# A planned pipeline on one core: first parts ordered by urgency with quantising beside the first early part, four banks in the last back part, step sizes one after the other, long steps in halves

## What is computed

```python
x = x + layernorm(attention(layernorm(x)))   # 2 heads, relu on q, k, v and on the output
x = x + layernorm(moe(layernorm(x)))         # 8 experts of 176, top 2, and a shared one; SwiGLU
x = x + layernorm(mamba(layernorm(x)))       # d_inner 512, 16 states, grouped B and C, conv of 4 taps
x = x + layernorm(ffn(layernorm(x)))         # relu squared, hidden 1024, rms norm, ternary weights
# mamba: delta = softplus(dt @ W_dt.T + 2 * b_dt)
#        state = exp(delta * A) * state + (delta * u) * B ;  y = sum over states of C * state
#        y = (y + u * D) * silu(z) ;  out = y @ W_out.T
# ternary weight: per 64 numbers scale = mean |w|, q = clip(round(w / scale), -1, 1) * scale
```

## Time and profile before

| | us |
|---|---|
| median of 3 runs | 1946.99 (1944.04 to 1947.22) |
| profiled execution, its own time | 1944.15 |
| its span | 1942.4 |
| busy: PE, DVE, ACT, POOL | 1609.7, 1521.5, 1198.9, 1000.3 |
| preamble and early(0) | 97.4 |
| late(0), early(1), quantising | 145.2 |
| iteration 0 | 193.8 |
| iterations 1 to 5 | 1053.1 (210.6 each) |
| iterations 6 and 7 | 203.4 and 157.7 |
| back(7) alone | 91.8 |

### The profile page before, as it was taken

One profiled execution on the slowest core, in us unless ns is written; L12 is line 12 of the kernel. 1 busy time (PEld: TensorE's weight loads), 2 busy tenths in 40 slices (PEclk: granted clock), 3 DMA queues, 4 the chain that ended last, 5 costly groups with the idle time before them and its releaser, 6 DMA issues. The chain is left out here.

```text
span 1942.4 us, 22619 instructions
## 1 busy us (share of the span) xinstructions
PE 1609.7 (83%) x5868; PEld 716.1 (37%) x5948; DVE 1521.5 (78%) x2808; ACT 1198.9 (62%) x2035; POOL 1000.3 (52%) x772
## 2 busy tenths in 40 slices
PE   2266488878997899979998899889997999789856
PEld 0113123323452346333552345234633354235224
DVE  5384599979998898969897998889986878586920
ACT  4347765677669575857577766957685536743421
POOL 0100645594449544764459444964477445864720
PEclk9987689879998899979998999989997899799988
DMA  4010022322223222322232222322232223232300
GB/s 117 2 48 22 25 85 95 111 80 79 92 92 110 73 85 77 121 77 75 87 107 81 87 88 85 115 73 90 71 121 77 82 92 119 75 111 93 123 1 11
DMA packets 94601, 157.95 MB, mean 81 GB/s; under 512 B 10940, under 2 KB 23660, under 8 KB 94468
## 3 DMA queue, kind: packets, MB, share of 16 engines
q1 hardware_dynamic: 94468, 156.43, 24.4%
HBM read 143.83 MB, written 12.58 MB: 81 GB/s over the span
## 5 line engine op out<-in xcount | busy, mean ns | idle before, releaser
L1401 POOL TENSOR_TENSOR prod<-state,c_all 128x512 f32<-128x512 f32 x512 | 653.0, 1280 | 550.5 <-DVE state L1378 436.1
L1378 DVE TENSOR_TENSOR_SCAN state<-decay,ps_b 128x512 f32<-128x512 f32 x512 | 621.8, 1214 | 53.3 <-ACT decay L1121 30.2
L924 PE MATMUL ps_y<-prod,idf 128*128 128x512 f32 x1024 | 606.2, 685 | 18.2 <-DVE u L1391 9.7
L1121 ACT ACTIVATE decay<-delta,a_neg 128x512 f32<-128x512 f32 x512 | 362.7, 721 | 222.6 <-DVE state L1378 221.9
L1385 DVE TENSOR_TENSOR ps_b<-du,ps_b 128x512 f32<-128x512 f32 x512 | 349.1, 682 | 87.2 <-PE ps_b L917 86.4
L917 PE MATMUL ps_b<-b_rows,sel_b 48*128 48x512 bf16 x512 | 207.3, 408 | 74.5 <-DVE state L1378 72.7
L924 PEld LDWEIGHTS ps_y<-prod,idf 128*128 128x128 f32 x1024 | 174.3, 203 | 165.1 <-issue 107.3
L917 PEld LDWEIGHTS ps_b<-b_rows,sel_b 48*128 48x128 bf16 x512 | 47.1, 93 | 376.5 <-DVE state L1378 234.0
L793 PE MATMUL ps_x<-xT,w 128*128 128x512 bf16 (+1 forms) x386 | 130.4, 417 | 30.7 <-DVE arena_l L1284 12.0
L896 PE MATMUL ps_x<-arena_b,fcT 128*128 128x512 f32 x256 | 125.4, 613 | 6.2 <-ACT arena_b L1103 5.5
L709 PE MATMUL ps_x<-hT,win 128*128 128x512 bf16 (+1 forms) x449 | 114.5, 388 | 13.3 <-DVE arena_b L1350 6.8
(11 more groups left out here) (236 smaller groups left out, 2411.1 us busy)
## 6 DMA issues: line engine op xcount, KB each, us to landing
c_all<-c_rows SPq DMA_DIRECT2D x512, 256.0 KB
c_rows<-arena_l SPq DMA_DIRECT2D x32, 256.0 KB
out<-arena_b SPq DMA_DIRECT2D x8, 512.0 KB
x_in<-in_base SPq DMA_DIRECT2D x8, 256.0 KB
c_all<-in_winT SPq DMA_DIRECT2D x1, 1280.0 KB, 7.1
arena_b<-in_w_fc SPq DMA_DIRECT2D x1, 1024.0 KB, 5.8
arena_b<-in_w_proj SPq DMA_DIRECT2D x1, 1024.0 KB, 4.7
w<-in_w1T SPq DMA_DIRECT2D x1, 792.0 KB, 5.8
```

The source lines that it names most:

```text
L924: nc.tensor.matmul(ps_y[:], idf[:], prod[:, n % NP, :], start=(n % NST == 0), stop=(n % NST == NST - 1)).then_inc(reduced, 1)
L1121: nc.scalar.activation(decay[:, n % NDA, :], delta[:, slot(s, ct), :], ACT.Exp, scale=a_neg[:, ct, st:st + 1]).then_inc(decayed, 1)
L1378: nc.vector.tensor_tensor_scan(state[:, n % NS, :], decay[:, n % NDA, :], ps_b[:, n % NDB, :], 0.0, ALU.mult, ALU.add).then_inc(scanned, 1)
L1401: nc.gpsimd.tensor_tensor(prod[:, n % NP, :], state[:, n % NS, :], c_all[:, n % NC, :], ALU.mult).then_inc(multiplied, 1)
```

## The change

1. **First parts.** `together`, `in_slots` and `COST` are gone. early(0) runs alone as before, and from round 24 of its 106 on (17 behind the `divide` of its first norm) the 30 quantising rounds are put behind its rounds at equal distances. Both weights are loaded with the other weights, ahead of w1, w3 and w2, each into a buffer of its own. Then `weave` orders late(0) (urgency 1000) and early(1) (urgency 1) until `du 0` is over, and the rest of both goes into iteration 0 as *held* chains, where late(1) and early(2) may start only when both are over. That iteration has weights of its own (`FIRST`).
2. **Last back part.** In back(7) the products of `wout`, `f_turn`, `fc`, `proj` and `gram` go to four banks by turns (`back_bank`), and their waits are those for the copy four products back.
3. **Step sizes.** The order of the blocks becomes 0, 3, 1, 2 (`D_ORDER`), and each has nine rounds of its own (15 + 9 k) instead of chains that begin at rounds 14, 15, 17 and 18.
4. **Halves.** `proj`, `gram`, `fc`, `wout`, `x4`, `apply`, the `add` of GpSimd and `gate_root` become two steps each (`first_half`, `halved`), and so does the store. Between the halves the planner can put steps of other chains.
5. **Planner.** New `BUSY`, table loads counted on their own (`TABLE_LOAD`), `decay` and `drive` know `delta` and `du` of their block, dependences name their batch element, new `URGENT`.

```diff
+D_ORDER = (0, CT - 1) + tuple(range(1, CT - 1))
+D_AT = tuple(D_ORDER.index(i) for i in range(CT))
...
-    d0 = (14, 15, 17, 18)
     for i in range(CT):
-        k = d0[i]
+        k = 15 + 9 * D_AT[i]
...
+FIRST_HALF = {"proj": "proj_a", "gram": "gram_a", "fc": "fc_a", "wout": "wout_a", "x4": "x4_a", "apply": "apply_a", "add": "add_a",
+              "gate_root": "gate_root_a"}
...
-URGENT = {"late": (0.32, 0.21, 0.17, 1.42, 0.34, 0.61, 0.01, 0.02),
-          "early": (10.39, 34.83, 6.82, 0.21, 3.35, 1.44, 0.16, 15.73),
-          "back": (17.26, 1.18, 330.85, 0.1, 0.06, 9.73, 0.79, 0.05),
-          "scan": (1.15, 30.65, 1781.42, 14, 0.66, 0.61, 1.19, 2.87)}
+URGENT = {"late": (1.07, 0.00728, 16.8, 1.59, 10.8, 0.0792, 0.106, 0.0435),
+          "early": (573, 12.7, 31.1, 1.48e+04, 2650, 36.1, 48.6, 3.13),
+          "back": (2.03, 102, 0.0246, 0.997, 0.832, 0.0938, 0.278, 0.712),
+          "scan": (3.58, 0.00555, 618, 1.07, 0.162, 0.27, 1e-05, 0.647)}
...
+        def back_bank(s, i):
+
+            return (XB, 0, 1, 2)[i % 4] if is_seq(s, NBATCH - 1) else XB
...
+                if D_AT[i] == 0:
+                    eng.wait_ge(late["V"], la(s, "V", ("u", CT - 1)))
+                elif D_AT[i] == 3:
+                    eng.wait_ge(late["A"], la(s, "A", ("d_abs", D_ORDER[0])))
...
+                    if back_bank(s, 1) == XB:
+                        free = ("f_turned", 1) if i == 0 else ("relu", i - 1)
+                    else:
+                        free = ("f_turned", 1) if i < 4 else ("relu", i - 4)
...
+        QUANT_FROM = place_of(EARLY, ("x", "divide")) + 17
...
+        def alone(e, eng, fns, chain, extra=None, beside=(), begin=0):
+
+            n = len(chain) - begin
             for k, rnd in enumerate(chain):
                 run_steps(e, eng, fns, rnd)
                 if extra is not None:
                     extra(k)
+                for m, more in enumerate(beside):
+                    if begin + m * n // len(beside) == k:
+                        run_steps(e, eng, fns, more)
...
+            if left >= 1:
+                chains.append(Chain(tagged("late", s.moved(1), LATE), urgent["late"], held))
+            if left >= 2:
+                chains.append(Chain(tagged("early", s.moved(2), EARLY), urgent["early"], held))
...
-            alone(e, eng, fns, tagged("early", Seq(0), EARLY), extra)
-            together(e, eng, fns, tagged("late", Seq(0), LATE), tagged("early", Seq(1), EARLY), tagged("quant", None, QUANT))
-            iteration(e, eng, fns, Seq(0), first=True)
+            alone(e, eng, fns, tagged("early", Seq(0), EARLY), extra, tagged("quant", None, QUANT), QUANT_FROM)
+            late0 = Chain(tagged("late", Seq(0), LATE), (1000,) * 8)
+            early1 = Chain(tagged("early", Seq(1), EARLY), (1,) * 8)
+            order, _ = weave([late0, early1], range(0), -1, (), (late0, place_of(LATE, ("du", 0)) + 1))
+            run_order(e, eng, fns, Seq(0), order)
+            late0.rest = [1e3 * x for x in late0.rest]
+            early1.rest = [1e6 * x for x in early1.rest]
+            iteration(e, eng, fns, Seq(0), (late0, early1))
```

More of the change, by code:

```diff
@@ L286 @@
+SCAN_BUSY = {"decay": 62, "spread": 33, "drive": 60, "scan": 114, "product": 123, "pair": 122, "sum": 96, "taken": 66, "load": 6}
+TABLE_LOAD = 128
+LOG_TABLE = ("log",)
+USES = {"d_log": "log", "gate_log": "log", "d_exp": "exp", "gate_exp": "exp", "exp": "exp", "decay": "exp",
+        "tanh": "tanh", "x_tanh": "tanh", "z_tanh": "tanh"}
 HANDOVER = 12
@@ L364, in head @@
     def head(self, e):
-        if self.at >= len(self.rounds):
+        if self.at >= len(self.rounds) or not all(chain.over() for chain in self.after):
             return None
@@ L1608, in alone, with run_order @@
                     extra(k)
[L1610 to L1627 removed]
+                for m, more in enumerate(beside):
+                    if begin + m * n // len(beside) == k:
+                        run_steps(e, eng, fns, more)
+        def run_order(e, eng, fns, s, order):
             for item in order[e]:
```

321 lines of the change are left out of this document (159 added, 162 removed).

## The result

The changed kernel takes **1934.37 us** (median of 6 runs, 1931.31 to 1938.25) against 1947.11 us for the kernel before beside it: a ratio of **0.9935** (95% interval 0.9918 to 0.9951). It is 0.65% faster, where 4% was forecast; the prediction is 66 us too low. The profiled execution took 1933.68 us, span 1931.9.

A forecast was written before the change was run, and what follows sets the result against it. TensorE and VectorE were taken to bound most of each iteration, GpSimd and a latency chain its end. First parts -25, loop -35, iterations 6 and 7 -6, last part -10.4: -76.4 from 1944.15, forecast 1868 us, range 1828 to 1920.

The forecast's parts named there:

- Near two bounds at once: Loop iterations: TensorE busy 191.8 and VectorE 183.8 of 210.6 us each; GpSimd and latency bind the end.
- Price of early(0): First early part: quantising steps put beside it lengthen it by 13 us (bounds 8 and 18).
- the 13 chunks: First late part, ahead of the first scan: 2.8 us each, 36.4 us, ending at about 147.
- The held chains: Start of iteration 0: over 42 us after the first scan, and only then may the next late and early parts start.
- the late chain needs about as long: Iteration 0: late chain taken to match VectorE's remaining 156 us, so 160, with the iteration ending at 411.
- Rival d: First parts give nothing: held chains only move work, iteration 0 grows by what its start gains; 1893 us, chance 0.07.
- the end behind `taken 2`: End of each loop iteration: fewer GpSimd steps there shorten 30.9 us to about 24, -6.5.
- the boundary: Gap between loop iterations: shrinks by 2 us, as no two step-size chains end there.
- their order can't be derived, and I take 0: Loop iterations: new urgency weights priced at 0 us (bounds -5 and +15).
- nothing in the middle: Loop iterations: what leaves the end comes back before it, where TensorE and VectorE are nearly full; 1908 us, chance 0.20.
- The rival of the late chains: Loop iterations: four serial step-size chains take 60 us; first `d` later than about 150 us loses; 1999 us, chance 0.09.
- Last part: Last back part: four banks save 7.9 us, halves of `add` and store the rest, -10.4 us (bounds -8 and -13).

The follow-up runs named there:

- e7: Changed kernel, same order, with `proj` making 2 of its 8 products, so less TensorE work: 1910.61 us, ratio 0.9795.
- e11: Changed kernel with the planner reckoning 11 instead of 12 units for a handover, same weights, so only the order differs: 2019.05 us, ratio 1.0368.
- e5: Kernel before with only the four banks of the last back part and the quantising moved beside the first early part: 1937.69 us, ratio 0.9942.
- e12: Changed kernel with step-size chains every five rounds instead of nine, planner counting 0.76 us for `drive`, `URGENT` and `FIRST` found anew: 1925.57 us, ratio 0.9880.
- e15: Changed kernel with step-size chains every five rounds, the planner's old scan cost, new weights with first `d` planned 2 us earlier: 1932.95 us, ratio 0.9926.
- e16: Changed kernel with step-size chains every five rounds, old scan cost, new weights with first `d` planned about 8 us earlier still: 1942.63 us, ratio 0.9973.
- e6: Changed kernel with late(0) and early(1) finished before the first scan, nothing held, `FIRST` kept: 1955.45 us, ratio 1.0033.
- e8: Changed kernel, same order, two more VectorE steps at each `center` and `divide` of early(2) to early(7): 1940.48 us, ratio 0.9959.
- e13: Changed kernel with other weights `URGENT` only, the first `d` planned 6 us earlier: 1928.15 us, ratio 0.9895.
- e14: Changed kernel with other weights only, the first `d` planned 17 us earlier at the price of later scans: 1981.76 us, ratio 1.0180.
- e1: Kernel before with only the four banks in the last back part: 1935.06 us, ratio 0.9932.
- e2: Changed kernel, same order, with the correction for rounding in the step-size chains made on 16 of 512 columns: 1916.27 us, ratio 0.9836.
- e3: Changed kernel, same order, with `proj` writing 32 of its 256 columns: 1924.86 us, ratio 0.9874.

## Why the prediction was wrong, and where it was right

**The bound.** Right as a reading (TensorE and VectorE near full up to `taken 2`, GpSimd and latency behind it), wrong as a cause. "Near two bounds at once" was taken to mean that what is freed at the end is won. In e7 11 us less of TensorE's work moved no loop iteration, and in e11 another order of the same work cost 17.6: a third thing holds, the order.

**Quantising.** Price of early(0) right (+10.4 against +13). That the stretch behind it wins in return was right too (-11.5 in e5), but then it is a move, and its gain is 1 us.

**First scan.** 210.8 against 209: right, but with luck, since two errors cancel. early(0) ended 2.7 us before its forecast, yet the 13 chunks ended at 153.6 instead of 147 (the `tanh` came every 3.3 us, not 2.8) and the first `d` at 197.6 instead of 192. The chain took 12.4 us (13 forecast), and the first scan came 0.8 us behind `du 0`, where 5 were put.

**Iteration 0.** 16.7 us too short. Two terms failed. The held chains took 50.3 us, not 42: the last `du` ended 43.7 us after the first scan, near the forecast, but the gate of early(1) is twelve small VectorE steps, most of them one or two scans apart in the order, and it ended last. And "the late chain needs about as long" as VectorE's work was wrong: it needed longer and ended in 34.3 us with next to no scan to fill them. In e12, e15 and e16, where the chains overlap (and `FIRST` is new), 14 of these 34.3 us go, and 7 us of the iteration with them. Rival d named the place (iteration 0 grows by 24.9, the first scan gained 31.8) and is wrong in part: e6, with nothing held, ends iteration 0 20 us later, how much of it by its weights is open.

**Loop iterations.** Of the -7 each, the end behind `taken 2` was right (-5.1 against -6.5, GpSimd 91% busy there and not under 80), the boundary gave 0.4 instead of 2. The failed step is the sentence that took 0 for the order and the urgency ("their order can't be derived, and I take 0"): the stretch before `taken 2` grew by 7.4 us on the mean, where 1.5 were put for collisions. That is the result of the rival *nothing in the middle* (rival a): what leaves the end comes back before it, in iteration 6 to within 0.4 us. Its mechanism, collisions of GpSimd with VectorE, may be there, as VectorE is busy 4.2 us more per iteration, but e8 makes it an unlikely cause. And its sum, 1908 us, is 26 us short too, 16.7 of them in iteration 0 and 9.6 in the loop. Which part of the change did it, the chains in a row, the halves or the weights, is not shown. The rival of the late chains had the place right, the first `d` at about 150 us, and near its point of decision, at 148.4 to 154.4 us, the iterations came out even. Its law, first `d` plus 60, held in four orders, and e11 is that rival come true. It broke in e13 and e14: in e13 the first `d_abs` comes 8 us earlier than in the changed kernel and the iteration is 1.7 us shorter. An early first `d` is not enough where the scans are put later for it.

**Collisions and table loads.** In the loop VectorE is busy 21.1 us more for the same work, and the rows below show steps that took the length of a product. By the Trainium skill, SBUF — State Buffer, section "Who interferes with whom", VectorE in a 2-port mode, or with two inputs in SBUF, and a reading GpSimd shut each other out for a whole instruction; the trace agrees, with 1.16 us for a step that took 0.15. e8 says that it hardly reaches the time. Table loads: 10 per loop iteration as before, each of 1.28 us, and the next activation starts 0.01 us behind it. The drain of 1.38 us that the Trainium skill, ScalarE: Activation LUTs, section "What ACT_TABLE_LOAD costs", puts behind a load is not seen in the loop of either kernel.

**Halves.** 0 in the loop can't be told apart from the rest; at the end they gave 0.7 to 2.9 us against 2.5 forecast.

**Last part.** -11.8 against -10.4. Right, and in sum it is the whole gain: e1 has nearly all of it alone (-9.5) and the same ratio. **Iterations 6 and 7.** Forecast -5 and -1; against e1 (199.8 and 157.3) they are +0.3 and +2.3.

What stays open: which property of an order decides. Neither the place of the first `d` nor the planner's cost of a scan does it alone, and what the changed weights would give with the chains of before was not tried.

## What to carry to other kernels

When a program fixes the order of all engines at build time, a saved microsecond can be worth nothing until the order is made again with it (11 us of TensorE in e7), or only what ends the iteration (2.6 us in e2). A moved one may be paid for where the order puts something else. Price such a change at the parts that run alone, and give the rest a range as wide as what orders of the same instructions differ by (here 17.6 us per iteration from one constant). Test it early: run one kernel with the same instructions in another order, and one with less work in the same order. And run one order in several profiled executions first: here five iterations of 1057 us varied by 9.

## What the runs showed of the hardware

Small VectorE steps that began just behind the start of a GpSimd product ended only with that product, up to 0.1 us behind it. In the loop of the changed kernel an addition on 128x4 took 1.16 us on the mean, where the trace of before has 0.15: all five began within 0.2 us after a product of 1.27 us did. `divide` of one site doubled: of its 20 steps five began just behind the start of a product and took 1.33 to 1.34 us, the other 15 took 0.26 to 0.28. First before, then after, groups of VectorE in the loop (count, busy us, mean ns):

```profile
L1339 DVE TENSOR_SCALAR ve_o<-rm 128x4 f32<-128x4 f32 x5 | 0.8, 154 | 0.0
L1156 DVE TENSOR_SCALAR arena_e<-arena_e,ri_a 128x256 bf16<-128x256 bf16 x20 | 4.4, 281 | 0.0
```

```profile
L1391 DVE TENSOR_SCALAR ve_o<-rm 128x4 f32<-128x4 f32 x5 | 5.8, 1160 | 0.0
L1206 DVE TENSOR_SCALAR arena_e<-arena_e,ri_a 128x256 bf16<-128x256 bf16 x20 | 9.5, 537 | 0.0
```

An f32 matmul does not fall with its columns in proportion: with 32 instead of 256 of them one instruction took 0.28 instead of 0.39 us, and 16 in a row 1.87 instead of 3.62 us (e3).
